# Fixed places for one chain of small steps in a two-layer cross attention, one unit combined in blocks, a lag of 116 steps in place of 124

## The chip, the cores and the metric

The kernel runs on one core of a Trainium2 chip. The metric is the time of one execution on the device in microseconds (us). TensorE (PE in the profile), VectorE (DVE), ScalarE (ACT), GpSimd (POOL) and SyncE (SP, which here only issues DMAs) run their own lists of instructions and meet at semaphores. A wait stands in its engine's list, so everything behind it in that list waits too.

## The reference

Two layers of cross attention with 20 heads of 16 columns, on 4 batches of 512 queries and 1024 keys. Everything is float32. Layer 0 is

```python
q, k_t, v_t = heads(x @ W_q), heads(text @ W_k), heads(text @ W_v)      # text: the first 1020 tokens
probs_t = softmax(q k_t / 4);  text_out = probs_t v_t
qsem = l2norm(probs_t @ text);  sem = qsem . l2norm(ip)                 # ip: the last 4 tokens
probs_ip = softmax(q k_ip / 4 + 0.5 * sem) * mask
x1 = (text_out + probs_ip v_ip) @ W_out + b_out + x
```

Layer 1 takes x1 and is simpler. It has two softmaxes, one over the first 77 tokens and one over the other 947 with other weights, and its output is (out_text + out_ip) @ Wo + bo + x1.

## The kernel before

**Units, groups, chunks.** A unit is one layer and one half batch of 256 queries (`UNITS`, line 52): units 0 to 7 are layer 0, units 8 to 15 are layer 1. `B` is 8, and `LAST` is unit 15. Unit 8 + b needs the output x1 of unit b. A unit has ten groups of two heads. A head has four chunks of 256 keys, so a unit has 80 chunks and the kernel has 1280. A chunk is scored on TensorE (the `score` step), ScalarE takes exp of it twice (`prob` and the rounded `prob_hi`), the difference `prob_lo` is formed on VectorE (layer 0, and one in eight of the tail) or on GpSimd (the rest of layer 1), and TensorE multiplies both parts with the values: `mix` in layer 0, which also forms the 512 columns of qsem, and `av1` in layer 1.

**The order.** `plan()` writes one list of steps, which all engines walk. `unit_sequence()` (line 62) interleaves the layers: layer 1 runs `LAG_UNITS` chunks behind layer 0. With 124 there are three phases: "lead" (124 chunks of layer 0 alone), "woven" (516 pairs of one chunk from each layer) and "tail" (chunks of layer 1 alone). I number the chunks of the whole order, n = 0 to 1279. Before, the tail begins with n = 1155 and has 125 chunks: 45 of unit 14 and the 80 of LAST. LAST begins at n = 1200, before and after. I write "tail + 8" for the eighth chunk after the tail's first one.

**Side work.** Between chunks `hook(limit)` takes up to `limit` steps, three in the tail: first what is in `urgent`, then `topq`, then `bgq`. `topq` is filled from `top_agenda`, a list by chunk number, which holds the maxima: for each group eight matmuls (`max`, line 1150) with a reduction on VectorE each (lines 1548, 1549 and 1551), then `neg`, `neg_parts` and `max_rows`, which put minus the row maxima beside the queries. A group's first score needs its `max_rows`. `bgq` is filled from `jobs` with deadlines, spread over windows of four chunks by `job_tasks()`. `put_off()` lets one small piece go per call of `hook`. `load_at` holds the places of `load_qk(g)`, which loads queries and keys of group g into a ring of five slots. If they aren't ready by then, `load_due()` runs the missing steps at once, all together. This happens once in the kernel before, at n = 1183 (tail + 28).

**The chain between the layers' last units.** When unit 7 ends, at the tail's start, these steps lead to LAST's queries: `combine` (lines 1606 to 1614), `fuse_root`, `fuse_exp` and `fuse_probs` (lines 1397, 1651 to 1688: the small softmax over four tokens), `probs_rows` (1257), three `turn` (1276, 1279, 1709, 1711), three `finish` (1297, 1719), `x_split` (1354, 1703) and three `q` (1176) with `split`, `split_hi` and `lower`, which cut q in three bf16 parts on VectorE and GpSimd and store them by DMA (1439 to 1449, 1737, 1743, 1835). `load_qk` of LAST's first group then reads them back (1870 to 1874). Before, these steps are a job in `bgq`. By the printed order `combine` stands at tail + 8 to + 10, `fuse_exp` at + 11 and + 12, `fuse_probs` up to + 16, `probs_rows` at + 17, `turn` at + 19 to + 24, `finish` at + 25 to + 27, `x_split`, the first `q`, its whole split and three `load_qk` together at + 28, the second `q` at + 32 and + 33, the maxima of LAST's first group at + 34 to + 39 with `max_rows` at + 40, its first score at + 42, and the third `q` at + 55.

**Unit 14.** After its last head (tail + 44) it is combined with seven put-off steps (lines 1610 to 1620, tail + 49 to + 51): two reciprocals, four multiplications of 320 columns and two additions of 320. LAST is combined in three blocks of 8, 8 and 4 heads (`combine_block`, lines 1632 to 1641), the first two while its heads are still running.

Of the kernel before, what the change touches and what calls it, by code (L numbers as in the profile page):

```python
# [7 lines left out]
ALU = mybir.AluOpType  # L8
# [7 lines left out]
HEADS = 20  # L16
# [4 lines left out]
SEM_SCALE = 0.5  # L21
LAG_UNITS = 124
WINDOW = 4
# [20 lines left out]
DH = D // HEADS  # L44
# [10 lines left out]
NU = NT // UNIT_KEYS  # L55
LAST = 2 * B - 1
BLOCKS = [(P * m // DH, (P * m + MW[m]) // DH) for m in range(NM)]
PER_GROUP = GROUP * NU
# [57 lines left out]
def plan():  # L116
# [280 lines left out]
    for g, (u, gi) in enumerate(seq):  # L397
        if g >= RING:
            done_at = end_of[g - RING] - (1 if end_of[g - RING] < woven else 2)
            at = max(done_at, start_of[g] - (25 if g < RING + 12 else 28 if start_of[g] < tail else 36))  # L400
            load_at.setdefault(max(at, start_of[place[(u, 0)]] - 16) if u == 2 * B - 1 else at, []).append(g)
        layer = UNITS[u][0]
        mine = [x for x in range(groups) if UNITS[seq[x][0]][0] == layer]
        i = mine.index(g)
        if i >= 2 or layer == 1:
            load_v_at.setdefault(max(end_of[mine[i - 2]] if i >= 2 else 0, start_of[g] - 24), []).append(g)
# [76 lines left out]
    def last_close():  # L483
# [9 lines left out]
        for m in range(NM):  # L493
            o.add("finish", LAST, m, NM - 1)

    def unit_done(u):
        layer, b = UNITS[u]
        if u == LAST:
            last_block(NM - 1)
            return  # L500
        put_off(*[("combine", u, i) for i in range(3 if layer == 0 else 7)])
        if layer == 0:
            add_job(project_q(B + b), due_of(B + b))
            if b + 2 < B:
                add_job(project_q(b + 2), due_of(b + 2))
            if b % PARTS == 1 and b + 3 < B:
                add_job(project_kv(b + 3), due_of(b + 3), "kv")
            if b % PARTS == 0 and b + 2 < B:
                add_job(project_kv(B + b + 2), due_of(B + b + 2), "kv")
        else:  # L510
            first, second = close(u)
            if u < LAST - 1:
                add_job(first + second, window_of(start_of[place[(u, 0)]] + 16 * PER_GROUP * NG // PER_GROUP))
            else:
                add_job(first + second, window_of(start_of[place[(LAST, 0)]] + 24))
# [41 lines left out]
    for g in range(1, groups):  # L557
        span, margin = MAX_SPAN[phase(start_of[g])]
        last_at = start_of[g] - margin
        if seq[g] == (2 * B - 1, 0):  # L560
# [27 lines left out]
    def rows_of(n):  # L588
        _, u, h, c = chunks[n]
        if n < 0 or UNITS[u][0] == 0 or c < NU - 1:  # L590
            return
        o.add("l1_rows", n)
        urgent.append((n + 3, lambda: turn_head(u, h)))
        if u == LAST and h + 1 in [end for _, end in BLOCKS[:-1]]:
            urgent.append((n + 5, lambda: last_block([end for _, end in BLOCKS].index(h + 1))))
        if h == HEADS - 1:
            urgent.append((n + 3, lambda: unit_done(u)))
# [44 lines left out]
    for n, (g, u, h, c) in enumerate(chunks):  # L642
# [22 lines left out]
        if layer == 0:  # L665
# [23 lines left out]
            if c == NU - 1:  # L689
                if h == 0:  # L690
                    drain()
                o.add("values", n, 0)
                values_due.append(n)
                if h == HEADS - 1:
                    urgent.append((n + 3, lambda u=u: unit_done(u)))
# [33 lines left out]
def cross_attention_pair(nc, a, out):  # L729
# [32 lines left out]
    with ctx:  # L762
# [149 lines left out]
        close0 = {s[1]: i for i, s in enumerate([s for s in o.steps if s[0] == "fuse_root"])}  # L912
        comb_base, comb_here, base = {}, {}, 0
        for s in o.steps:
# [5 lines left out]
            elif s[0] == "combine_block":  # L920
                comb_base.setdefault(s[1], base)
                base += 2 if s[3] == 0 else 1
        ip_nth = {s[1]: i for i, s in enumerate([s for s in o.steps if s[0] == "ip_norm"])}
        head_end = {(u, h): n for n, (g, u, h, c) in enumerate(chunks) if c == NU - 1}
# [109 lines left out]
        def _(e):  # L1034
# [16 lines left out]
            for s in o.steps:  # L1051
# [207 lines left out]
                elif kind == "turn":  # L1259
# [4 lines left out]
                    if k == 0:  # L1264
                        e.wait_ge(s_comb, comb_base[u] + (5 * (m + 1) if u == LAST else COMBINED[layer]))
                        if layer == 0:
# [136 lines left out]
        def _(e):  # L1403
            for x, rows in ((x_in[1], high_rows), (o_t[1], low_rows)):
                e.memset(x.bitcast(F32)[rows, NM - 1, :], 0.0).then_inc(s_pad, 1)
            for s in o.steps:
# [214 lines left out]
                elif kind == "combine_block":  # L1621
                    _, u, m, piece = s
                    h0, h1 = BLOCKS[m]
                    i0 = comb_base[u] + 5 * m
                    ho = heads_out[1][:, :, h0:h1, :]
# [7 lines left out]
                    elif piece == 1:  # L1633
                        e.wait_ge(s_comb, i0 + 1)
                        e.tensor_tensor(at, ho[:, :, :, 0:DH], wide[0], ALU.mult).then_inc(s_comb, 1)
                    elif piece == 2:
                        e.wait_ge(s_comb, i0 + 2)
                        e.tensor_tensor(image, image, wide[1], ALU.mult).then_inc(s_comb, 1)
                    else:
                        e.wait_ge(s_comb, i0 + 4)  # L1640
                        e.tensor_tensor(at, at, image, ALU.add).then_inc(s_comb, 1)
                elif kind == "fuse_exp":
                    _, u, piece = s
# [121 lines left out]
        def _(e):  # L1765
            for s in o.steps:
# [137 lines left out]
                elif kind == "residual":  # L1904
                    _, u, m = s
                    layer, b = UNITS[u]
                    w, nth_close = MW[m], close_nth[u]
                    e.wait_ge(s_comb, comb_base[u] + (5 if u == LAST else COMBINED[layer]))
                    if nth_close:
# [58 lines left out]
```

## Time and profile before

| | us |
|---|---|
| median of 3 runs | 3438.0 (3437.28 to 3439.05) |
| the profiled execution's own time | 3436.6 |
| its span in the trace | 3434.8 |
| TensorE busy | 3332.4 (97%) |
| VectorE, ScalarE, GpSimd busy | 1994.1, 1832.6, 1089.5 |

Busy times are those of the span. An engine's busy share doesn't say what the end waits for, so the page's slices come next, and then the trace of the last 200 us. A line number is that of the kernel before.

### The profile page before, as it was taken

How to read it: one execution, taken by the hardware profiler on the slowest of the kernel's cores; microseconds unless marked ns; L12 is line 12 of the kernel's file. 1: busy time of each engine (PE TensorE's matmuls, PEld its weight loads, DVE VectorE, ACT ScalarE, POOL GpSimd, SP SyncE). 2: the span in 40 equal slices, each digit the busy share in tenths (PEclk: the TensorE clock that was granted, in tenths of full speed). 3: DMA queues.
4: the chain of work that ended last, by engine and by line, in shares of the span. 5: the costliest groups of instructions: out<-in, count | busy, mean ns of one | idle time of the engine just before them, and what ended most of it. 6: DMA issues, size and time to landing. Idle time of an engine off the chain costs nothing.

```text
span 3434.8 us, 65575 instructions
## 1 busy us (share of the span) xinstructions
PE 3332.4 (97%) x24736; PEld 2893.0 (84%) x24736; DVE 1994.1 (58%) x5511; ACT 1832.6 (53%) x4006; POOL 1089.5 (32%) x932
## 2 busy tenths in 40 slices
PE   6999999999999999999999999999999999999978
PEld 3888978887888888888888888888888898989755
DVE  4444455556655566565656556655665556555677
ACT  2333334555555555555655555555565566565668
POOL 2111010234332333333433232333423322322368
PEclk8999999999999999999999999999999999999989
DMA  6333822233358332233347432323327532222232
GB/s 186 108 87 71 97 84 76 62 80 90 86 79 105 77 74 68 75 92 81 92 72 72 98 73 68 78 72 104 90 68 76 67 59 51 59 47 53 49 79 57
DMA packets 648781, 271.28 MB, mean 79 GB/s; under 512 B 479666, under 2 KB 599426, under 8 KB 648468
## 3 DMA queue, kind: packets, MB, share of 16 engines
q1 hardware_dynamic: 648468, 267.10, 38.0%
q8 instruction: 198, 3.24, 0.4%
q14 instruction: 115, 0.94, 0.1%
HBM read 187.97 MB, written 79.04 MB: 78 GB/s over the span
## 4 chain that ended last, share of the span: by engine, by line
PE 88%; DVE 5%; ACT 3%; POOL 1%; issue 1%; DMA 1%; SPq 1%; POOLq 0%; ACTq 0%; DVEq 0%
PE acc L1106 9%; PE acc L1099 9%; PE acc L1102 8%; PE acc L1101 8%; PE acc L1107 8%; PE acc L1100 7%; PE score L1066 4%; PE spare L1150 4%; PE score L1150 4%; PE score L1068 4%; PE av L1141 3%; PE av L1137 3%; PE spare L1191 2%; PE score L1191 2%; PE score L1240 2%; PE spare L1240 2%
## 5 line engine op out<-in xcount | busy, mean ns | idle before, releaser
L1317 ACT ACTIVATE prob<-score 128x512 f32<-128x512 f32 x1219 | 729.1, 598 | 1194.2 <-PE score L1068 1189.0
L1731 POOL TENSOR_TENSOR prob_lo<-prob,prob_hi 128x512 fp32r<-128x512 f32 x624 | 811.9, 1305 | 1487.3 <-ACT prob_hi L1320 1486.8
L1099 PE MATMUL acc<-tok_v,prob_hi 128*128 128x300 f32 x2240 | 908.6, 406 | 0.9 <-issue 0.9
L1101 PE MATMUL acc<-tok_lo,prob_hi 128*128 128x256 f32 (+1 forms) x2560 | 757.9, 296 | 0.0
L1106 PE MATMUL acc<-tok_v,prob_lo 128*128 128x278 f32 (+1 forms) x2560 | 745.5, 291 | 0.0
L1320 ACT ACTIVATE prob_hi<-score 128x512 fp32r<-128x512 f32 x1219 | 726.2, 596 | 0.0
L1102 PE MATMUL acc<-tok_lo,prob_hi 128*128 128x256 f32 (+1 forms) x2560 | 719.0, 281 | 0.0
L1107 PE MATMUL acc<-tok_v,prob_lo 128*128 128x256 f32 (+1 forms) x2560 | 717.8, 280 | 0.0
L1100 PE MATMUL acc<-tok_v,prob_hi 128*128 128x256 f32 x2240 | 627.6, 280 | 0.0
L1102 PEld LDWEIGHTS acc<-tok_lo,prob_hi 128*128 128x128 f32 (+1 forms) x2560 | 483.6, 189 | 7.4 <-issue 1.4
L1101 PEld LDWEIGHTS acc<-tok_lo,prob_hi 128*128 128x128 f32 (+1 forms) x2560 | 484.4, 189 | 4.1 <-issue 1.8
L1106 PEld LDWEIGHTS acc<-tok_v,prob_lo 128*128 128x128 f32 (+1 forms) x2560 | 482.4, 188 | 0.0
L1107 PEld LDWEIGHTS acc<-tok_v,prob_lo 128*128 128x128 f32 (+1 forms) x2560 | 481.7, 188 | 0.0
L1430 DVE TENSOR_TENSOR prob_lo<-prob,prob_hi 128x512 fp32r<-128x512 f32 x656 | 461.9, 704 | 30.4 <-ACT prob_hi L1320 29.7
L1099 PEld LDWEIGHTS acc<-tok_v,prob_hi 128*128 128x128 f32 x2240 | 427.9, 191 | 44.4 <-issue 20.2
L1100 PEld LDWEIGHTS acc<-tok_v,prob_hi 128*128 128x128 f32 x2240 | 427.7, 191 | 35.1 <-issue 17.2
L1066 PE MATMUL score<-q_ring,k_ring 99*128 99x256 bf16 (+1 forms) x1219 | 337.9, 277 | 15.1 <-ACT prob_hi L1320 14.3
L1068 PE MATMUL score<-q_ring,k_ring 99*128 99x256 bf16 (+1 forms) x1219 | 330.9, 271 | 0.0
L1137 PE MATMUL av<-prob_hi,v_ring 128*33 128x256 f32 (+1 forms) x1152 | 273.2, 318 | 4.1 <-issue 4.1
L1150 PE MATMUL spare<-k_ring,q_ring 96*128 96x512 bf16 x605 | 237.3, 392 | 5.6 <-DVE max_parts L1551 2.6
L1141 PE MATMUL av<-prob_lo,v_ring 128*33 128x256 f32 (+1 forms) x1152 | 230.5, 281 | 5.5 <-POOL prob_lo L1731 4.5
L1150 PE MATMUL score<-k_ring,q_ring 96*128 96x512 bf16 x586 | 229.8, 392 | 4.4 <-DVE max_parts L1549 2.3
(323 smaller groups left out, 4963.5 us busy)
## 6 DMA issues: line engine op xcount, KB each, us to landing
k_ring<-k_scr SPq DMA_DIRECT2D x160, 384.0 KB
tok_v<-v_scr SPq DMA_DIRECT2D x158, 176.0 KB, 3.4
v_ring<-v_scr SPq DMA_DIRECT2D x160, 148.5 KB, 3.4
ctx_t<-in_ctxT SPq DMA_DIRECT2D x16, 1024.0 KB, 8.7
q_ring<-q_scr SPq DMA_DIRECT2D x160, 96.0 KB
v_scr<-v_stage SPq DMA_DIRECT2D x32, 440.0 KB, 2.6
v_scr<-v_stage SPq DMA_DIRECT2D x36, 330.0 KB, 9.3
tok_stage<-in_ctx SPq DMA_DIRECT2D x32, 256.0 KB, 3.0
```

The source lines that it names most:

```text
L1066: e.matmul(score[n][:, 0:SQ], k_ring[0:depth, slot, j, 2 * c * P:(2 * c + 1) * P], queries, start=True, stop=True)
L1068: e.matmul(score[n][:, SQ:2 * SQ], k_ring[0:depth, slot, j, (2 * c + 1) * P:(2 * c + 2) * P], queries, start=True, stop=True).then_inc(s_s ...
L1099: e.matmul(out_a[:, 0:SEG + VCOLS], p_hi, tok_v[0:kk, c, seg, v_lo:v_lo + SEG + VCOLS], start=first, stop=False)
L1100: e.matmul(out_b[:, t0:t0 + SEG], p_hi, tok_v[0:kk, c, 1 - seg, VCOLS:VCOLS + SEG], start=first, stop=False)
L1101: e.matmul(out_a[:, t0:t0 + SEG], p_hi, tok_lo[0:kk, c, seg * SEG:(seg + 1) * SEG], start=False, stop=False)
L1102: e.matmul(out_b[:, t0:t0 + SEG], p_hi, tok_lo[0:kk, c, (1 - seg) * SEG:(2 - seg) * SEG], start=False, stop=False)
L1106: e.matmul(out_a[:, v_one:v_one + SEG + VH], p_lo, tok_v[0:kk, c, seg, v_lo + v_one:v_lo + v_one + SEG + VH], start=False, stop=False)
L1107: mm = e.matmul(out_b[:, t0:t0 + SEG], p_lo, tok_v[0:kk, c, 1 - seg, VCOLS:VCOLS + SEG], start=False, stop=False)
L1150: e.matmul(bg[:, :], q_ring[0:96, slot, j, st * P:(st + 1) * P], k_ring[0:96, slot, j, half * 512:(half + 1) * 512], start=True, stop=True ...
L1317: e.activation(prob[:, es, :], bank_s[:, :], ACT.Exp, scale=SCALE)
L1320: e.activation(prob_hi[:, ps, :], bank_s[:, :], ACT.Exp, scale=SCALE).then_inc(s_exp, 1)
L1731: e.tensor_tensor(prob_lo[:, ps, :], prob[:, es, :], prob_hi.bitcast(F32)[:, ps, :], ALU.subtract).then_inc(s_low[1], 1)
```

## The change

It has five parts. First, `LAG_UNITS` is 116: lead 116 chunks, woven 524 pairs, tail 117 chunks (n = 1163 to 1279), 37 of them of unit 14. Second, the chain above is no job any more. `last_chain()` puts each step at a fixed chunk: `combine` 0, `fuse_root` and two `fuse_exp` at tail + 1, the other two at + 2, `combine` 1 and `fuse_probs` 0 at + 3, `combine` 2 and `fuse_probs` 1 at + 4, `fuse_probs` 2 at + 5, the residual loads at + 6, `probs_rows` at + 7, `turn` at + 8 to + 10, `finish` at + 11 to + 13, `x_split` at + 15, `q` at + 17 to + 19. Third, unit 14 is combined in blocks like LAST, but the additions are done at the end, as two `combine_sum` steps of 320 columns each, since `attn` still holds unit 7 when the blocks begin. Fourth, the maxima of unit 14's groups that start in the tail are due 11 chunks ahead of the group's start in place of 14. Fifth, LAST's loads of queries and keys stand 12 chunks ahead of its start at the earliest in place of 16 (n = 1188), and those of unit 8, the first of layer 1, at most 14 ahead.

```diff
-LAG_UNITS = 124
+LAG_UNITS = 116
+BY_BLOCKS = (LAST - 1, LAST)
...
-            load_at.setdefault(max(at, start_of[place[(u, 0)]] - 16) if u == 2 * B - 1 else at, []).append(g)
+            load_at.setdefault(max(at, start_of[place[(u, 0)]] - (12 if u == LAST else 14)) if u in (B, LAST) else at, []).append(g)
...
+    def last_chain():
+
+        u = B - 1
+        tasks = [t for t in project_q(LAST) if not isinstance(t, Pause)]
+        root, exps, (ask, total, probs), rows = tasks[0], tasks[2:6], tasks[7:10], tasks[11]
+        (res0, res1, res2), turns, finishes = tasks[12:15], tasks[15:18], tasks[18:21]
+        x_split, q = tasks[22], tasks[23:]
...
+        places = [(0, several(lambda: combine(0), root, *exps[0:2])), (1, several(*exps[2:4])),
+                  (2, several(lambda: combine(1), ask)), (3, several(lambda: combine(2), total)), (4, probs),
+                  (5, several(res0, res1, res2)), (6, rows)]
+        places += [(7 + m, turns[m]) for m in range(NM)] + [(10 + m, finishes[m]) for m in range(NM)]
+        places += [(14, x_split)] + [(16 + m, q[m]) for m in range(NM)]
+        for at, task in reversed(places):
+            top_agenda.setdefault(now[0] + 2 + at, []).insert(0, task)
...
-        put_off(*[("combine", u, i) for i in range(3 if layer == 0 else 7)])
+        if u in BY_BLOCKS:
+            put_off(*[("combine_block", u, NM - 1, i) for i in range(3)], *[("combine_sum", u, st) for st in range(ST)])
+        else:
+            put_off(*[("combine", u, i) for i in range(3 if layer == 0 else 7)])
...
-        last_at = start_of[g] - margin
+        last_at = start_of[g] - (11 if start_of[g] >= tail and seq[g][0] == LAST - 1 else margin)
...
-        if u == LAST and h + 1 in [end for _, end in BLOCKS[:-1]]:
-            urgent.append((n + 5, lambda: last_block([end for _, end in BLOCKS].index(h + 1))))
+        if u in BY_BLOCKS and h + 1 in [end for _, end in BLOCKS[:-1]]:
+            m = [end for _, end in BLOCKS].index(h + 1)
+            if u == LAST:
+                urgent.append((n + 5, lambda: last_block(m)))
+            else:
+                urgent.append((n + 5, lambda: put_off(*[("combine_block", u, m, i) for i in range(3)])))
...
-                if h == HEADS - 1:
+                if u == B - 1 and h == HEADS - 1:
+                    last_chain()
+                elif h == HEADS - 1:
                     urgent.append((n + 3, lambda u=u: unit_done(u)))
...
+                        text = ho[:, :, :, 0:DH]
+                        e.tensor_tensor(at if u == LAST else text, text, wide[0], ALU.mult).then_inc(s_comb, 1)
...
+                elif kind == "combine_sum":
+                    _, u, st = s
+                    ho = heads_out[1][:, st, :, :]
+                    e.wait_ge(s_comb, comb_base[u, NM - 1] + 4)
+                    e.tensor_tensor(attn[:, st, :, :], ho[:, :, 0:DH], ho[:, :, DH:2 * DH], ALU.add).then_inc(s_comb, 1)
```

The rest of the diff keeps count of the semaphore `s_comb` for the blocks of two units.

## Rows read from the trace of the kernel before

**Rows 1.** The page: busy time by engine; TensorE and its granted clock in 40 slices.
```profile
PE 3332.4 (97%) x24736; PEld 2893.0 (84%) x24736; DVE 1994.1 (58%) x5511; ACT 1832.6 (53%) x4006; POOL 1089.5 (32%) x932
...
PE   6999999999999999999999999999999999999978
...
PEclk8999999999999999999999999999999999999989
```

**Rows 2.** Windows of the tail: stretch, length, busy time of each engine, clock, DMA.
```profile
core 0: us, PE busy (x) PEld busy (x) DVE busy (x) ACT busy (x) POOL busy (x), PEclk, DMA share, GB/s
...
3245.00:3267.00 22.00, 14.19 (x81) 8.64 (x81) 21.03 (x59) 15.81 (x31) 12.82 (x11) 0.84 0.15 30
...
3287.00:3297.00 10.00, 7.73 (x55) 6.35 (x56) 2.45 (x8) 5.75 (x12) 6.76 (x6) 0.83 0.35 96
3297.00:3305.00 8.00, 3.87 (x29) 2.60 (x28) 5.18 (x11) 4.88 (x10) 7.27 (x7) 0.88 1.03 212
...
3327.00:3334.00 7.00, 1.95 (x9) 0.98 (x8) 6.90 (x12) 1.47 (x5) 3.97 (x3) 0.75 0.56 123
...
3341.00:3398.00 57.00, 53.14 (x390) 35.19 (x389) 54.14 (x163) 54.51 (x114) 53.70 (x43) 1.00 0.38 75
```

**Rows 3.** TensorE's timeline: `av1` of tail + 0, 5, 18, 29, 45, 61, 105.
```profile
3236.40 0.48 PE L1137 MATMUL av<-prob_hi,v_ring 128*33 128x256 f32 x2
...
3241.35 0.48 PE L1137 MATMUL av<-prob_hi,v_ring 128*66 128x256 f32 x2
...
3267.85 0.48 PE L1137 MATMUL acc<-prob_hi,v_ring 128*33 128x256 f32 x2
...
3288.03 0.48 PE L1137 MATMUL av<-prob_hi,v_ring 128*66 128x256 f32 x2
...
3316.86 0.48 PE L1137 MATMUL av<-prob_hi,v_ring 128*66 128x256 f32 x2
...
3345.31 0.47 PE L1137 MATMUL av<-prob_hi,v_ring 128*66 128x256 f32 x2
...
3398.48 0.48 PE L1137 MATMUL acc<-prob_hi,v_ring 128*66 128x256 f32 x2
```

**Rows 4.** TensorE's waits from 3236 to 3340: total us, times, longest.
```profile
PE acc L1150 <- DVE heads_out L1593: 4.9, 1, 4.9
PE av L1137 <- issue: 4.1, 1, 4.1
...
PE spare L1150 <- DVE max_parts L1551: 2.6, 1, 2.6
PE spare L1176 <- DVE x_in_lo L1703: 2.6, 1, 2.6
```

**Rows 5.** Windows, VectorE alone, of tiles `max_parts`, `small` and `w`.
```profile
3245.00:3267.00 22.00, 8.75 (x22) 0.84 0.15 30
...
3245.00:3268.00 23.00, 8.05 (x14) 0.85 0.15 29
...
3245.00:3268.00 23.00, 1.82 (x4) 0.85 0.15 29
```

**Rows 6.** VectorE's timeline: unit 14's combination, first and last of its rows.
```profile
3324.13 0.40 DVE L1610 RECIPROCAL small<-heads_out 128x40 f32<-128x40 f32 x1
...
3328.30 3.02 DVE L1617 TENSOR_TENSOR heads_out<-heads_out,small 128x320 f32<-128x320 f32 x2
3331.35 1.02 DVE L1620 TENSOR_TENSOR attn<-attn,heads_out 128x320 f32<-128x320 f32 x2
```

**Rows 7.** One line over the span: shortest, median and longest duration in ns.
```profile
L1614 DVE TENSOR_TENSOR attn<-heads_out,small x30: 472/482/1599, 430.7 to 3327.4; 128x320 f32<-128x320 f32 x30
...
L1638 DVE TENSOR_TENSOR heads_out<-heads_out,small x3: 286/1494/1497, 3413.4 to 3428.0; 128x256 f32<-128x256 f32 x2, 128x128 f32<-128x128 f32 x1
```

**Rows 8.** Timelines of SP's queue and TensorE: LAST's first group, load, maximum, score.
```profile
3293.49 0.28 SPq L1870 DMA_DIRECT2D k_ring<-row_scr  x1
...
3297.85 0.39 PE L1150 MATMUL score<-k_ring,q_ring 96*128 96x512 bf16 x1
...
3313.70 0.27 PE L1066 MATMUL score<-q_ring,k_ring 102*128 102x256 bf16 x1
```

More of the change, by code:

```diff
@@ L494, in last_close, with combine, several, go @@
             o.add("finish", LAST, m, NM - 1)
+    def last_chain():
[4 more added lines that the diff above has]
+        x_split, q = tasks[22], tasks[23:]
+        def combine(i):
+            o.add("combine", u, i)
+        def several(*tasks):
+            def go():
+                for task in tasks:
+                    task()
+            return go
+        places = [(0, several(lambda: combine(0), root, *exps[0:2])), (1, several(*exps[2:4])),
[5 more added lines that the diff above has]
+            top_agenda.setdefault(now[0] + 2 + at, []).insert(0, task)
     def unit_done(u):
@@ L912, in cross_attention_pair @@
         close0 = {s[1]: i for i, s in enumerate([s for s in o.steps if s[0] == "fuse_root"])}
-        comb_base, comb_here, base = {}, {}, 0
+        comb_base, comb_done, comb_here, base = {}, {}, {}, 0
         for s in o.steps:
@@ L920, in cross_attention_pair @@
             elif s[0] == "combine_block":
-                comb_base.setdefault(s[1], base)
+                comb_base.setdefault(s[1:3], base)
                 base += 2 if s[3] == 0 else 1
+                comb_done[s[1:3]] = base
+            elif s[0] == "combine_sum":
+                base += 1
+                comb_done[s[1], NM - 1] = base
         ip_nth = {s[1]: i for i, s in enumerate([s for s in o.steps if s[0] == "ip_norm"])}
@@ L1264, in _ @@
                     if k == 0:
-                        e.wait_ge(s_comb, comb_base[u] + (5 * (m + 1) if u == LAST else COMBINED[layer]))
+                        e.wait_ge(s_comb, comb_done[u, m if u == LAST else NM - 1] if u in BY_BLOCKS else comb_base[u] + COMBINED[layer])
                         if layer == 0:
@@ L1623, in _ @@
                     h0, h1 = BLOCKS[m]
-                    i0 = comb_base[u] + 5 * m
+                    i0 = comb_base[u, m]
                     ho = heads_out[1][:, :, h0:h1, :]
@@ L1634, in _ @@
                         e.wait_ge(s_comb, i0 + 1)
-                        e.tensor_tensor(at, ho[:, :, :, 0:DH], wide[0], ALU.mult).then_inc(s_comb, 1)
+                        text = ho[:, :, :, 0:DH]
+                        e.tensor_tensor(at if u == LAST else text, text, wide[0], ALU.mult).then_inc(s_comb, 1)
                     elif piece == 2:
@@ L1907, in _ @@
                     w, nth_close = MW[m], close_nth[u]
-                    e.wait_ge(s_comb, comb_base[u] + (5 if u == LAST else COMBINED[layer]))
+                    e.wait_ge(s_comb, comb_done[u, 0 if u == LAST else NM - 1] if u in BY_BLOCKS else comb_base[u] + COMBINED[layer])
                     if nth_close:
```

## The prediction, made before the changed kernel was built

> **What bounds the kernel now.** I read the page's busy times and slices first [rows 1]. TensorE is busy 97% of the span, and its slices are all at 9 except the first and the last two. So until the tail the kernel is bound by TensorE's own work, and an edit that only moves work about in the woven phase gives nothing there. The last two slices stand at 7 and 8 with a lower clock, and the whole change acts on them.
>
> Then I read the tail's windows and its chunks. `av1` of the tail's first chunk starts at 3236.40 and of tail + 45, LAST's first chunk, at 3316.86 [rows 3]: 80.5 us for 45 chunks, 1.79 each. From tail + 61 to + 105 it is 53.17 us for 44 chunks, 1.21 each, with ScalarE busy 54.51 of 57 us, VectorE 54.14 and GpSimd 53.70 [rows 2, 3]. All three are full there, so 1.21 is the tail's free pace. The first five chunks take 4.95 us, 0.99 each [rows 3]: that is TensorE's own pace, since the scores are ahead. At 1.21 the 45 chunks would take 54.5 us, so 26 us are lost before LAST starts. Another 9.1 us are lost in the 16 chunks behind it (28.45 us in place of 19.4).
>
> The losses have four places. (1) From 3245 to 3267 VectorE is busy 21.03 of 22 us [rows 2], with both the maxima and the chain's small steps. (2) TensorE waits 2.6 us for `x_split`'s low part, which stands right ahead of `q` in the bunch that `load_due()` forces, and 4.1 us at an `av1`, just when SP issues the loads of three groups ahead of the values; DMA is at 1.03 in that window [rows 2, 4]. (3) The clock falls to 0.83 and 0.88 of full between 3287 and 3305 [rows 2]. (4) TensorE waits 4.9 us for `heads_out` while VectorE combines unit 14: it is busy 1.95 of 7 us there and VectorE 6.90 [rows 2, 4].
>
> **The change part by part.** I sum against the profiled execution: span 3434.8, 3436.6 with what lies around it, 1.4 under the median.
>
> *Eight chunks leave the tail for the woven phase.* There each costs TensorE's pace, 8 x 0.99 = +7.9 us. The same chunks and side work remain in total, and the lead phase loses eight chunks of layer 0 that become halves of pairs, at the same TensorE work. What they cost in the tail is in the stretches below. Below nothing this can't be, since TensorE is at 9 in nearly every slice there; its upper bound is the tail's free pace, 8 x 1.21 = 9.7.
>
> *Stretch A, the tail's start to `probs_rows`.* Before it was 18 chunks and 31.45 us, 3236.40 to 3267.85 [rows 3]. After it is 7 chunks. VectorE sets it. Its chain steps cost 8.05 us on `small` and 1.82 on `w`, with one operation of 0.3 in both: 9.5 us [rows 5]. The rest of VectorE's 21.03 us, 11.5 us, belongs to the ten chunks from tail + 8 to + 18, 1.15 each, 8.75 of it maxima [rows 2, 5]. Seven chunks then make 7 x 1.15 + 9.5 = 17.6, and I take 18. It can't be under 17.0 (nothing is left out of the chain and the maxima go on at one per chunk; their later due time takes three at most away). The upper bound is 24: the steps now stand back to back, and TensorE, in order, may wait at a bank for a maximum that stands behind three of them.
>
> *Stretch B, from there to the first `q`.* Eleven chunks before (20.2 us, 3267.85 to 3288.03 [rows 3]) and eleven after. `x_split` now stands two chunks ahead of `q`, which covers 2 x 1.21 us of work; since side steps slip by a chunk or so when more than three are due, I take half of the 2.6 us wait [rows 4]. The maxima of the unit's last two groups now lie beside it, which I put at +0.5. 19.4 us; bounds 17.6 (the wait wholly gone) and 23 (as before, and four maxima more at 0.7).
>
> *Stretch C, from there to LAST's first chunk.* 16 chunks before and 28.8 us; 19 after. At the free pace 23.0. The 4.1 us at `av1` go: the values of the group that waited are loaded ahead of the three `load_qk` now, not behind. What is late next is LAST's first group. Its load stands nine chunks ahead of the step that scores it: 10.9 us of cover. In the trace, load to first maximum is 4.4 us and load to first score 20.2 [rows 8], of which 4.1 is that wait. The least is 4.4 + 8 x 0.73 (maxima at 8.75 us for some twelve [rows 5]) = 10.2, the most 16.1. So TensorE waits between 0 and 5.2 us for `max_rows`; 3.4, above the middle, because all eight maxima become due in one chunk. Block 1 of unit 14's combination lands here too, where VectorE is busy 2.45 of 10 us [rows 2]: nothing; without that cover it would cost its some 3 us (two operations of 1.5 [rows 7]). C is 26.4; bounds 23.0 and 33.
>
> A + B + C = 63.8 in place of 80.5: -16.7 us.
>
> *Unit 14 in blocks.* Before, its steps fill VectorE from 3324.13 to 3332.4, 8.2 us [rows 6]. After, the last four heads and two sums remain: two small reciprocals (under 0.4 each, by that of 40 columns), two multiplications of 128 columns (0.29 at the shortest, 1.50 at the longest [rows 7]) and two sums (1.02 for both in rows 6, up to 1.6 each [rows 7]). That makes 1.9 to 7.0 us; I take 3.0, near the short end, as the sums were at 0.5 in this same place. So -5.2; bounds -6.3 and -1.2. What is late behind it is the free pace. The block of the first eight heads falls into the woven phase, where VectorE has 40% free.
>
> The same operation takes 472 ns at the shortest and 1599 at the longest [rows 7], and the long ones lie where GpSimd is full. The Trainium skill, GPSIMD Engine Reference, Specifications, says that GpSimd shares its SBUF interfaces with VectorE and collides with operations of two SBUF inputs; all of the combination's multiplications and sums are such. By that rule the last block alone would take up to 7.0 us in the tail, and the sum would come out 4 us higher. The row with 472 ns shows that it isn't so each time. The rule is one of the reasons for the first rival.
>
> *The rest.* The loads of unit 8 change nothing, since their deadline falls on the same window as before (chunk 100, now 102). From LAST's seventeenth chunk on, the order of steps stays, and its 89.5 us with it.
>
> Sum: 7.9 - 16.7 - 5.2 = -14.0. The execution comes to 3422.6, the median to 3424.0 us.
>
> **The rivals.** *The chain stays in-order bound.* Packing the steps doesn't make VectorE faster; TensorE waits at more banks and more `max_rows`, and GpSimd stretches the two-input operations. Against it: VectorE is busy only 2.45 of 10 and 5.18 of 8 us from 3287 to 3305 [rows 2], which the fixed places can fill. A = 24, B = 22, C = 29 give 75, -5.5; blocks -5.2; +7.9: -2.8, that is 3435.
>
> *Slower: LAST's first group comes late.* Place: `max_rows` of LAST's first group, scored nine chunks behind its loads in place of thirteen. If load to score takes the 20.2 us of rows 8 in place of the cover's 10.9, TensorE waits 9.3 us. With the loads behind the stores of the second and third `q` on SP's queue, A = 26 and B = 24 (a little above their bounds, for the lower clock behind long waits) and C = 23.0 + 3.7 for these stores + 9.3 = 36, the tail's first part takes 86 us: +5.5 + 7.9 - 5.2 = +8.2, 3446. It decides from 85 us between the tail's first chunk and LAST's first. For it speaks that DMA was full when these loads ran [rows 2]; against it that the bunch then held three groups and values behind a forced `q`, all of which are apart now.
>
> *More than forecast.* The stalls go nearly all: A + B + C at 37 x 1.21 + 9.5 = 54, -26.5; -5.2; +7.9: -24, 3414. It needs VectorE to work the chain wholly beside the chunks, while it has 2.9 of 57 us free at that pace [rows 2].
>
> *It doesn't do what it says.* The fixed places are places in `topq`, and three steps per chunk are let through. With maxima, head turns and chain that is passed from tail + 8 on, so steps may slip two to three chunks. That costs no more than the first rival and is in it.
>
> **How the numbers follow.** Forecast 3424, chance 0.58, with an own range of 3418 to 3431. First rival 3435: 0.19. Slower 3446: 0.11. More 3414: 0.12. Some 7 us (0.2%) is about what a measurement of this kernel can tell from no change, so faster ends at 3431 and slower begins at 3445: faster 0.70, same 0.19, slower 0.11. The range leaves out the slower rival and a part of the best one: 3413 to 3438.
>
> **What would show it.** In the trace of the changed kernel: 117 `av1` behind the last `mix`; LAST's first chunk 60 to 68 us after the tail's first, `probs_rows` near 18 us; the wait of 4.1 us at `av1` and that of 4.9 us for `heads_out` gone; a wait of `max_rows` of 2 to 5 us right ahead of LAST; clock above 0.9 but for single windows; unit 14's last block and sums in 2 to 4 us; the pace from then on 1.21 us per chunk and the last 64 chunks in 89.5 us. The forecast is wrong if the first stretch takes over 24 us, if LAST's first score comes later than 85 us, or if the woven phase grows by more than 9.7 us.

## The result, and the profile after

The changed kernel takes 3475.6 us (median of 4 runs, 3467.7 to 3476.9) against 3438.5 (3437.3 to 3439.9) before: a ratio of 1.0104 with an interval of 1.0091 to 1.0116. It is slower by 37 us, where 14 faster was forecast. The profiled execution took 3476.9 us, its span is 3475.1. The page of the changed kernel, busy times and TensorE's slices:

```profile
PE 3354.0 (97%) x24736; PEld 2905.7 (84%) x24736; DVE 1991.3 (57%) x5516; ACT 1835.8 (53%) x4006; POOL 1094.0 (31%) x933
...
PE   6999999999999999999999999999999999999978
...
PEclk8999999999999999999999999999999999999989
```

Against [rows 1] nothing is to be seen but 22 us more of TensorE. So I cut the order at steps that mean the same in both kernels: layer 0's chunk 124 (counted from 0), the tail's first chunk and LAST's first one. I give all kernels of this study by this cut, in us from the span's start to chunk 124, from there to the tail, from the tail to LAST, and from LAST's first chunk to its last output matmul.

| kernel | median | ratio to before, interval | to chunk 124 | to the tail | to LAST | LAST |
|---|---|---|---|---|---|---|
| before | 3438.5 | | 629.4 | 2607.0 | 80.5 | 114.6 |
| after | 3475.6 | 1.0104 (1.0091 to 1.0116) | 637.5 | 2650.4 | 73.1 | 110.8 |
| `lag116_alone` | 3479.0 | 1.0120 (1.0105 to 1.0135) | 636.5 | 2654.4 | 74.9 | 113.1 |
| `lag116_no_blocks` | 3472.3 | 1.0103 (1.0085 to 1.0121) | 636.6 | 2643.6 | 74.0 | 112.1 |
| `lag116_kv_as_before` | 3458.3 | 1.0058 (1.0043 to 1.0072) | 637.9 | 2631.2 | 72.8 | 110.3 |
| `lag116_late_loads` | 3443.6 | 1.0016 (1.0007 to 1.0026) | 637.4 | 2618.2 | 70.8 | 110.7 |
| `lag116_late_due14` | 3434.9 | 0.9988 (0.9979 to 0.9998) | 637.0 | 2618.6 | 63.2 | 110.8 |
| `lag116_late_due14_kv` | 3433.0 | 0.9984 (0.9976 to 0.9993) | 636.9 | 2614.1 | 63.8 | 112.0 |
| `lag120_due14` | 3446.8 | 1.0024 (1.0015 to 1.0033) | 627.9 | 2624.9 | 78.5 | 110.6 |
| `lag124_chain_only` | 3433.7 | 0.9987 (0.9977 to 0.9996) | 630.0 | 2607.1 | 79.6 | 113.7 |
| `lag124_unit8_loads` | 3432.9 | 0.9987 (0.9977 to 0.9996) | 620.4 | 2612.1 | 82.9 | 114.8 |
| `lag124_rest_new` | 3430.1 | 0.9975 (0.9966 to 0.9985) | 619.7 | 2611.7 | 82.6 | 112.3 |
| `lag124_due14` | 3427.6 | 0.9969 (0.9957 to 0.9981) | 620.7 | 2612.0 | 77.4 | 112.0 |
| `lag128_due14` | 3460.4 | 1.0064 (1.0050 to 1.0078) | 625.0 | 2630.3 | 90.1 | 111.5 |

Between before and after these four stretches differ by 8.1 + 43.4 - 7.4 - 3.8 = 40.3 us, which is the growth of the span. The 8.1 us up to chunk 124 are the forecast 7.9 for eight chunks woven in. The 43.4 us behind it (43.3 by the windows below), in a stretch where the same work runs in both, had no term. Medians are of several executions, but each stretch is of one profiled execution. Three of the kernels (after, `lag116_alone` and `lag116_no_blocks`) have the same printed order up to chunk n = 1144, nearly the whole woven stretch, and still take 2650.4, 2654.4 and 2643.6 us there. So differences of ten us between woven stretches can be chance.

**The woven stretch.** Its window, first of the kernel before, then of after (length; busy time of TensorE, its loads, VectorE, ScalarE, GpSimd; clock, DMA):

```profile
629.40:3236.40 2607.00, 2585.46 (x19668) 2279.12 (x19667) 1541.69 (x4266) 1465.61 (x3196) 856.86 (x717) 1.00 0.37 75
```

```profile
638.00:3288.30 2650.30, 2603.09 (x19665) 2288.67 (x19664) 1540.05 (x4266) 1466.91 (x3195) 858.55 (x717) 0.99 0.37 74
```

The number of matmuls is the same, but for three that a trace misses. TensorE is idle for 47.2 us in place of 21.5, and busy 17.6 us longer for the same work. Its longest waits in that stretch, before and after (line waited at, what released it; total us, times, longest):

```profile
PE score L1066 <- ACT prob_hi L1320: 12.0, 13, 1.2
PE spare L1150 <- DVE max_parts L1549: 2.6, 4, 0.8
PE score L1150 <- DVE max_parts L1549: 1.9, 3, 0.7
```

```profile
PE score L1104 <- ACT prob_hi L1358: 19.8, 10, 6.0
PE score L1214 <- DVE x_in_lo L1747: 6.4, 3, 2.1
PE spare L1214 <- DVE x_in_lo L1747: 4.4, 2, 2.3
PE spare L1188 <- DVE max_parts L1587: 2.7, 5, 0.8
PE score L1288 <- DVE closing L1763: 2.5, 1, 2.5
```

Two kinds are new: five waits of a unit's first `q` for the low part of x, and two long waits (6.0 and 4.9 us) of a score for ScalarE.

*The first kind.* The timeline of after where unit 9 gets its queries:

```profile
907.81 0.93 ACT L1392 ACTIVATE x_in_hi<-closing 128x512 fp32r<-128x512 f32 x2
...
908.47 1.68 DVE L1747 TENSOR_TENSOR x_in_lo<-closing,x_in_hi 128x512 fp32r<-128x512 f32 x2 [1.54 <-ACT x_in_hi L1392]
...
910.41 0.47 PE L1214 MATMUL score<-x_in_hi,wq_parts 128*128 128x256 f32 x2 [2.12 <-DVE x_in_lo L1747]
```

`q` stands directly behind `x_split` in the list, so TensorE, in order, waits until ScalarE and VectorE have split all of x. By the printed order, before one step of mixing stood between the two only for unit 8, and 5 to 30 for units 9 to 14. After it is one for all but unit 10, which has four and is the one that doesn't wait. The woven phase has six such chains, one for each unit b of layer 0 whose x1 makes unit 8 + b's queries. The deadline of each is the load of unit 8 + b's first group. A lag of 116 puts that load 22 chunks of layer 0 behind the end of unit b (and the first score 35), where 124 puts it at 30 (and 43). To meet it, the job runs without room between its steps; run 4 below tests this.

*The second kind.* ScalarE at a border between batches, where the tokens of the next batch are read and split, and SP's queue ahead of it:

```profile
1682.13 0.63 ACT L1408 ACTIVATE tok_v<-tok_stage 128x512 fp32r<-128x512 f32 x1 [5.01 <-DMA tok_stage<-in_ctx]
...
1669.36 1.59 SPq L1943 DMA_DIRECT2D tok_stage<-in_ctx  x2
1671.49 0.53 SPq L1900 DMA_DIRECT2D v_scr<-v_stage  x1
1674.40 1.57 SPq L1943 DMA_DIRECT2D tok_stage<-in_ctx  x2
1676.08 0.29 SPq L1914 DMA_DIRECT2D k_ring<-row_scr  x1
1676.41 0.33 SPq L1916 DMA_DIRECT2D k_ring<-k_scr  x1
1676.78 2.42 SPq L1918 DMA_DIRECT2D q_ring<-q_scr  x1
```

And in the kernel before, at the same border:

```profile
1630.21 7.00 SPq L1899 DMA_DIRECT2D tok_stage<-in_ctx  x4
```

Before, all four token reads stand together; after, a store of values (`v_scr`) stands among them, since unit 12's value job now runs from layer 0's chunk 296 to 329 in place of 340 to 368, over the border at 317 to 320. ScalarE waits 5.0 us for a read, the exp of the next chunks stand behind that wait on its list, and TensorE waits 6.0 us for `prob_hi`. The same happens at 2535 us with unit 14. That the value jobs bring it is shown by run 5. What in them makes the read late isn't: the store ahead of it in the queue took 10.4 us to land, but the second pair of reads was also issued only 5.0 us after the first.

*The clock.* Windows of after around two of these waits (same columns):

```profile
905.00:912.00 7.00, 4.88 (x40) 4.55 (x40) 4.25 (x14) 3.44 (x8) 1.27 (x1) 0.99 0.35 62
912.00:916.00 4.00, 4.00 (x24) 3.99 (x24) 0.97 (x4) 1.41 (x3) 0.00 (x0) 0.59 0.00 0
1680.00:1687.00 7.00, 1.04 (x5) 0.79 (x5) 1.07 (x2) 3.37 (x9) 3.75 (x3) 0.74 0.65 150
1687.00:1691.00 4.00, 4.00 (x18) 3.38 (x17) 1.27 (x7) 1.92 (x4) 2.52 (x3) 0.61 0.64 144
```

Behind the wait TensorE is busy without a break, at a clock near 0.6, that is mostly at 1.2 GHz. The trace has seven stretches at 1.2 GHz in the woven phase after, 30.7 us in all, and none before: four at waits for the low part, two at the waits for ScalarE, and one at the wait of 2.5 us for `closing`. TensorE is busy in 25.8 of these us; at half speed half of that is lost, some 12.9 of the 17.6 us that it was busy longer. So the 43.3 us are 25.7 of waiting and 17.6 of slower work, and most of the second goes with the first.

### The profile page after: what moved, and what is told of

The parts are those of the page before. It is cut to its first block, busy times and chain, and to the rows that moved or that the text cites. A ratio compares the mean times of both kernels' runs of the same rounds, so it can differ in the third digit from the quotient of the medians.

```text
span 3475.1 us, 65594 instructions
## 1 busy us (share of the span) xinstructions
PE 3354.0 (97%) x24736; PEld 2905.7 (84%) x24736; DVE 1991.3 (57%) x5516; ACT 1835.8 (53%) x4006; POOL 1094.0 (31%) x933
## 4 chain that ended last, share of the span: by engine, by line
PE 86%; DVE 5%; ACT 2%; DMA 2%; issue 1%; SPq 1%; POOL 1%; POOLq 0%; DVEq 0%; ACTq 0%
PE acc L1144 9%; PE acc L1137 9%; PE acc L1139 8%; PE acc L1140 8%; PE acc L1145 8%; PE acc L1138 7%; PE score L1104 4%; PE spare L1188 4%; PE score L1188 4%; PE score L1106 4%; PE av L1175 3%; PE av L1179 3%; PE spare L1229 2%; PE score L1229 2%; PE score L1278 2%; PE spare L1278 2%
```

## The experiments

All start from the changed kernel, unless "before" is named. The times are in the table above.

**1. `lag124_rest_new`: everything but the lag.**

```diff
-LAG_UNITS = 116
+LAG_UNITS = 124
```

> The changed kernel with the lag set back to 124, all else of the change kept. Theory S (the shorter lag squeezes the chain from unit b to unit 8+b in every unit of the woven phase, so that each q stands right behind its x_split and TensorE waits and drops to the lower clock; the tail's edits are sound): the 2 us waits of the first q for x_in_lo in the woven phase are gone, at most one stretch of half clock there, tail begins at 3236 +- 3, and the time is 3438 less most of the 11 us that the changed tail gained: 3425 to 3433. Rival T (the other edits, the blocks above all, cost the woven phase its 43 us): 3465 or more.

3430.1 us. The woven stretch falls from 2650.4 to 2611.7 us, its waits for `prob_hi` are 11.6 us, and it has no stretch at 1.2 GHz. The other four parts together gain 0.25% (interval 0.15 to 0.34), and the lag costs 45 us on top of them, of which 17.8 lie ahead of chunk 124: 8 for the chunks woven in, and a gain of unit 8's loads that only the longer lag has (run 6).

**2. `lag116_alone`: before, with the lag and the rule for unit 8's loads.**

```diff
-LAG_UNITS = 124
+LAG_UNITS = 116
...
-            load_at.setdefault(max(at, start_of[place[(u, 0)]] - 16) if u == 2 * B - 1 else at, []).append(g)
+            load_at.setdefault(max(at, start_of[place[(u, 0)]] - (16 if u == LAST else 14)) if u in (B, LAST) else at, []).append(g)
```

> The kernel before with the lag of 116 and only the rule for unit 8's loads that this lag needs; chain, combination and maxima as before. Theory S: the woven phase loses its 40 to 45 us here too, with the q waits at x_in_lo and half-clock stretches; the tail has the forced bunch at tail + 20, so in all 3478 to 3495. Rival T: 3430 to 3445.

3479.0 us: the lag alone brings the whole loss, with the same waits and the same stretches at 1.2 GHz in the woven phase. Eight chunks fewer make the way from the tail to LAST only 5.6 us shorter (74.9 in place of 80.5).

**3. `lag116_no_blocks`: unit 14 combined whole.**

```diff
-BY_BLOCKS = (LAST - 1, LAST)
+BY_BLOCKS = (LAST,)
```

> The changed kernel with unit 14 combined whole as before. Theory S: the woven phase as in the changed kernel; behind LAST's first chunk the combination of 7 to 8 us on VectorE and a wait of TensorE for a head turn or a maximum of 4 to 5 us are back: 3476 + 2 to 6 us. Rival T: the woven phase is back at the level of before, 3430 to 3445.

3472.3 us, whose interval overlaps the changed kernel's, where I had expected 2 to 6 more. TensorE's wait ahead of the maxima of LAST's third group is 3.8 us in place of 2.5, and the tail as a whole is 2.2 us longer (186.1 in place of 183.9). The forecast 5.2 us aren't there. Two of this run's five waits for the low part were followed by a stretch at 1.2 GHz, where after has four.

**4. `lag116_late_loads`: the loads of units 9 to 14 at most 16 chunks ahead.**

```diff
-            load_at.setdefault(max(at, start_of[place[(u, 0)]] - (12 if u == LAST else 14)) if u in (B, LAST) else at, []).append(g)
+            load_at.setdefault(max(at, start_of[place[(u, 0)]] - (12 if u == LAST else 14 if u == B else 16)) if u >= B else at, []).append(g)
```

> The changed kernel with the loads of units 9 to 14 held until 16 steps ahead of the unit's first chunk, which moves their jobs' deadlines back by six chunks of layer 0, so that x_split and q stand apart as with the lag of 124. Theory S: the waits for x_in_lo in the woven phase fall from six of 2.1 us to one or two, half-clock stretches from eight to three or fewer, and the time to 3430 to 3450. Rival U (the half clock and the waits come from DMA at the batches' borders and not from the squeezed chain): 3465 or more, with the waits of 5 to 6 us of score for prob_hi left and the clock still low behind them.

3443.6 us, 32 fewer, all of it in the woven stretch (2618.2). The load now stands 28 chunks behind the end of unit b in place of 22, with 4 to 30 steps of mixing between `x_split` and `q` of units 9 to 14. The waits at `q` are gone from the list of the woven stretch, one stretch at 1.2 GHz is left, and TensorE is busy 2589.6 us. The deadline of the chain was the cause, not the chunks that moved. But which of the two kinds of wait weighs how much can't be told from it, since the same edit moves the value jobs of units 12 and 14 back behind the borders (from chunks 340 and 488). The next run parts the two. Some 11 us of the 43 stay here (2618.2 us against 2607.0), and 7 in run 11; no run says where they come from.

**5. `lag116_kv_as_before`: only the key and value jobs of units 12 and 14 moved back.**

```diff
-                add_job(project_kv(B + b + 2), due_of(B + b + 2), "kv")
+                add_job(([Pause(10)] if b else []) + project_kv(B + b + 2), due_of(B + b + 2), "kv")
```

> The changed kernel, where the jobs for the keys and values of units 12 and 14 are held back ten windows, so that they run beside the same chunks of layer 0 as in the kernel before (keys 300 to 320 and 460 to 480, values 340 to 364 and 500 to 535) and no longer across the batches' borders at 317 to 320 and 477 to 480. The q chains stay squeezed. Two-cause theory (waits of 6.0 and 4.9 us of score for prob_hi at the borders, and the squeezed q chains with 2 us each, are separate): the two border waits and their 13.6 us of half clock go, the six q waits stay, and the time falls by 14 to 24 us, to 3452 to 3462. Rival (the squeezed chain causes both): 3470 or more. Rival (the borders are nearly all): under 3448.

3458.3 us, 17 fewer, within the 14 to 24 of the theory with two causes. The woven stretch of this kernel, and its first waits:

```profile
638.10:3269.40 2631.30, 2592.73 (x19665) 2281.18 (x19664) 1548.35 (x4266) 1468.65 (x3195) 857.82 (x717) 1.00 0.36 74
```

```profile
PE score L1104 <- ACT prob_hi L1358: 9.2, 9, 1.3
PE score L1214 <- DVE x_in_lo L1747: 8.5, 4, 2.1
PE spare L1214 <- DVE x_in_lo L1747: 4.2, 2, 2.1
```

The two long waits for ScalarE are gone, and the six at `q` are all there, 12.7 us. They are followed by only one stretch at 1.2 GHz (at 910 us), where the changed kernel had four behind its five. So what a wait of 2.1 us brings behind it isn't settled by its length alone.

**6. `lag124_unit8_loads`: before, with unit 8's loads at most 14 chunks ahead.**

```diff
-            load_at.setdefault(max(at, start_of[place[(u, 0)]] - 16) if u == 2 * B - 1 else at, []).append(g)
+            load_at.setdefault(max(at, start_of[place[(u, 0)]] - (16 if u == LAST else 14)) if u in (B, LAST) else at, []).append(g)
```

> The kernel before with one edit alone: unit 8's loads of queries and keys at most 14 steps ahead. Theory E (of the 8 us that the changed kernel gains at a lag of 124, the part before the tail, 5 us in the profiled runs, comes from this rule, because unit 8's chain stops being packed behind one deadline): layer 0's chunk 100 starts near 506 us in place of 526, the tail at 3231 to 3233, and the time is 3430 to 3434. Rival (it is the tail's edits or chance): 3437 to 3440.

3432.9 us, a gain of 0.13% (0.04 to 0.23). Chunk 124 comes 9.0 us earlier, and 5.1 of them come back in the woven stretch. The waits of TensorE from 300 to 510 us in the kernel before were these; with the rule there are none.

```profile
PE av L1161 <- DVE row_parts L1582: 2.6, 2, 1.6
PE av L1176 <- DVE x_in_lo L1703: 1.3, 1, 1.3
PE av L1297 <- DVE o_t_lo L1711: 0.2, 1, 0.2
```

By the printed order the rule moves unit 8's first load from 19 to 30 chunks of layer 0 behind the end of unit 0, and 20 steps of mixing then stand between `x_split` and `q` in place of one. With a lag of 116 the same rule leaves `x_split` at chunk 96 and one step of mixing, as before, and the changed kernel has the same waits from 300 to 510 us: 4.0 us in place of 4.1.

**7. `lag116_late_due14`: run 4, with unit 14's last maxima due 14 chunks ahead, as before.**

```diff
-        last_at = start_of[g] - (11 if start_of[g] >= tail and seq[g][0] == LAST - 1 else margin)
+        last_at = start_of[g] - margin
```

> lag116_late_loads with unit 14's maxima due 14 chunks ahead as before, not 11. Theory M (the later due time makes max_rows of the last groups late, 3.2 us of wait at the group 149): that wait falls under 1 us, and the time is 3 us less, near 3440. Rival N (VectorE has the same maxima in either case and the wait only moves to the chain): within 1.5 us of 3443.6, with a longer stretch from the tail's start to probs_rows than 18.4 us.

3434.9 us, 8.7 fewer than run 4, where I had put 3. From the tail to LAST it is 63.2 us in place of 70.8. The wait that goes is that of `max_rows` for group 149, unit 14's last, 3.2 us in the changed kernel; the clock's stretches at 1.2 GHz in the tail up to LAST shrink from 17 us (run 4) to 10. By the printed order `neg`, `neg_parts` and `max_rows` of this group stand in one chunk (tail + 25), right ahead of its first score, when the maxima are due 11 ahead; with 14, `neg` stands four chunks ahead. This part of the change costs time.

**8. `lag124_chain_only`: before, with the fixed places alone** (`last_chain()` as in the diff ahead of the prediction).

> The kernel before with the fixed places for the chain alone (lag 124, unit 14 combined whole, maxima due 14 ahead, loads of LAST as before, no rule for unit 8). Theory P (with 45 chunks to go through before LAST the stretch is bound by VectorE and ScalarE work, not by the chain's latency, so an earlier chain gains little): tail to LAST's first chunk 78 to 83 us, time 3434 to 3439. Rival L (the chain was what LAST waited for): 70 us or less and 3428 or less.

3433.7 us, a gain of 0.13% (0.04 to 0.23). `probs_rows` comes at 16.6 us in place of 31.1, the first `q` at 39.2 in place of 50.5, but LAST's first chunk only 0.9 us earlier (79.6). The time goes back in waits, among them those of `max_rows` for groups 149, 150 and 151 (1.8, 2.0 and 2.2 us, the last one behind LAST's first chunk), each with a stretch at 1.2 GHz beside it. The fixed places take the chain off the path, and the maxima take it over.

**9. `lag124_due14`: run 1 with run 7's edit.**

> All of the change but the lag (124 stays), and unit 14's last maxima due 14 steps ahead, as before the change, in place of 11. Theory (the later due place only makes TensorE wait at the last maxima, and each such wait is followed by a stretch at 1.2 GHz): the stretch from the tail's start to the last unit's first chunk falls from 82.6 us to 74 to 79, and the median from 3430.1 to 3422 to 3427. Rival (what the 116-step kernel gained by it, 8.7 us by its span, came from the places that steps took there by chance): within 2 us of 3430.1.

3427.6 us, the fastest of the study: 0.31% under before (0.19 to 0.43). The way from tail to LAST falls from 82.6 to 77.4 us, within the 74 to 79 of the theory, though the median falls by only 2.5, half a microsecond short of the forecast band, and the span by 4.3.

**10. `lag120_due14`: the same with a lag of 120.**

> The same with a lag of 120. Theory (the eight chains from a unit of layer 0 to layer 1's unit lose half of the room that 116 steps take): between the two, chunks moved into the woven phase add 4 us there and take 4 to 6 off the tail, and waits of TensorE of more than 1.3 us ahead of queries appear in at most some units: 3420 to 3432. Rival (any cut of the room brings the waits of 2 us and the stretches at 1.2 GHz back): three or more stretches at 1.2 GHz in the woven phase and over 3440.

3446.8 us, over the theory's 3432. The rival has the time right, but not its reason: there is one stretch at 1.2 GHz in the woven phase, and two waits of 2.1 us at `q`. What is new are waits of maxima:

```profile
PE score L1188 <- DVE max_parts L1581: 4.5, 4, 1.5
PE spare L1214 <- DVE x_in_lo L1747: 4.3, 2, 2.1
PE spare L1188 <- DVE max_parts L1581: 3.0, 3, 1.3
```

**11. `lag116_late_due14_kv`: run 7 and run 5's pause together.**

> The change with the loads of units 9 to 14 held to 16 steps ahead, unit 14's last maxima due 14 steps ahead, and a pause of 10 chunks ahead of the key and value jobs of units 12 and 14. Theory (held loads and moved value jobs are two remedies for the same waits, so the second finds little left): 3431 to 3437, beside 3434.9 without the pauses; the two stretches at 1.2 GHz in the woven phase (near 1911 and 2311 us) go or stay one. Rival (each takes away waits of its own): below 3430.

3433.0 us. The median is 1.9 us lower, within overlapping intervals, and the stretches at 1.2 GHz near 1911 and 2311 us are gone. As expected the second remedy finds little left. So held loads had mended both kinds of wait.

**12. `lag128_due14`: run 9 with a lag of 128.**

> All of the change but the lag, which is 128, and unit 14's last maxima due 14 steps ahead. By its printed order only three to six steps of mixing stand between a unit's low part of x and its first query (one at 116, 5 to 30 at 124, 1 to 25 at 120). Theory (those steps are what hides the low part; each such place without cover costs up to 2.1 us, and four chunks go back from the woven phase to the tail, 4 us less there and 5 to 7 more here): waits at the queries of 0.5 to 1.5 us at four or more units, 3428 to 3438, over the 3427.6 of lag 124. Rival (a longer lag only gives the chains more room, whatever stands where): no waits over 0.5 us at the queries, and 3427 to 3431.

3460.4 us, over both expectations. The queries don't wait more (0.9 us at one unit), though only three to six steps of mixing hide the low part; so few are enough, and one is not. The woven stretch is 18 us longer than with 124 for another reason, and the tail 13 us. Its waits of maxima:

```profile
PE spare L1188 <- DVE max_parts L1581: 4.3, 3, 1.5
PE score L1188 <- DVE max_parts L1581: 4.1, 3, 1.5
PE spare L1188 <- DVE max_parts L1587: 3.0, 2, 1.8
PE score L1199 <- DVE row_parts L1620: 2.8, 2, 2.2
```

At 124 the waits at line 1188 in the woven stretch come to 5.1 us with 0.8 at the longest; at 120 they are 12.7, at 128 15.4. At these lags the maxima of layer 1 fall beside other steps of layer 0. Which ones, no run parts.

## Why the prediction was wrong

**Eight chunks to the woven phase (+7.9).** The step that failed. The eight chunks themselves cost 8.1 us, as worked out. What was put at nothing behind them measures 43.4. What I wrote behind it, "its upper bound is the tail's free pace, 9.7", bounded the chunks that move and not what a new lag does to the rest. The lag is the distance between unit b and unit 8 + b in every place, so it shortens six more chains and the jobs filed with them, not only the one that the change gives fixed places. My first reading, that an edit which only moves work in the woven phase gives nothing, since TensorE is at 9 in every slice [rows 1], took a busy engine for one that can't be delayed. It was already idle 21.5 us there, in 2607. What the slices can't show is how near each hand-over stands. I had listed the chain's places only for unit 7, and the same list for units 1 to 6 would have shown one step of cover in place of 5 to 30 (four for unit 10). That wait was in my rows too: `x_in_lo`, 2.6 us [rows 4], for just that standing, `q` right behind `x_split`.

**Stretch A (18).** `probs_rows` comes 18.4 us behind the tail's first chunk, but that was luck in part: the fixed places are places in the queue, and steps slipped behind the maxima. By the printed order and the trace `probs_rows` runs at tail + 9 and not + 7, and the sum's own prices give 19.9 us for nine chunks. **Stretch B (19.4)** took 22.2, within its bounds of 17.6 to 23, for twelve chunks and not eleven: `x_split` runs at tail + 20 (place + 15) and the three `q` at + 21, + 24 and + 25 (places + 17 to + 19). So one chunk stood between `x_split` and `q`, not two, and the wait for the low part came at 2.0 us with a first matmul at half clock. **Stretch C (26.4)** took 32.5, at its upper bound of 33, though only 16 chunks were left for it in place of 19. At the free pace they are 19.4 us, so 13 us were lost where the sum had 3.4. Timeline of after, the `av1` of the tail's first chunk, the first `q`, and LAST's first `av1`:

```profile
3287.86 0.47 PE L1175 MATMUL av<-prob_hi,v_ring 128*33 128x256 f32 x2
...
3328.46 0.71 PE L1214 MATMUL score<-x_in_hi,wq_parts 128*128 128x256 f32 x2 [2.04 <-DVE x_in_lo L1747]
...
3360.92 0.48 PE L1175 MATMUL av<-prob_hi,v_ring 128*66 128x256 f32 x2
```

A, B and C are 73.1 in place of 63.8 us. The largest mis-sized term is that of the maxima due later: "at + 0.5", where run 7 measures 7.6. TensorE's waits in the tail of after:

```profile
PE acc L1199 <- DVE row_parts L1620: 3.4, 2, 3.2
PE score L1199 <- DVE row_parts L1620: 2.6, 1, 2.6
...
PE spare L1188 <- DVE heads_out L1631: 2.5, 1, 2.5
PE spare L1199 <- DVE row_parts L1620: 2.2, 1, 2.2
PE score L1214 <- DVE x_in_lo L1747: 2.0, 1, 2.0
```

The wait of 4.1 us at `av1` is gone, as forecast. In place of two `max_rows` waits of 1.4 and 1.3 us (groups 150 and 151) there are three, of 3.2, 2.6 and 2.2 us, for groups 149, 150 and 151; the last one is behind LAST's first chunk, as before. And I had costed waits without the clock behind them: windows of the tail of after show 0.73 to 0.89 where I had forecast over 0.9.

```profile
3308.00:3330.00 22.00, 19.70 (x137) 16.52 (x136) 13.70 (x40) 15.78 (x32) 13.96 (x11) 0.89 0.24 44
3330.00:3345.00 15.00, 11.12 (x72) 8.57 (x71) 9.15 (x27) 8.12 (x16) 9.01 (x11) 0.73 0.38 106
3345.00:3362.00 17.00, 12.70 (x77) 7.84 (x76) 13.54 (x33) 10.61 (x23) 11.08 (x10) 0.88 0.63 137
```

**Unit 14 in blocks (-5.2).** TensorE's wait for `heads_out` fell from 4.9 us [rows 4] to 2.5, and LAST's first 16 chunks take 28.0 in place of 28.45 us, so most of the term is absent. VectorE and GpSimd in after:

```profile
3368.21 0.27 DVE L1670 RECIPROCAL small<-heads_out 128x8 f32<-128x8 f32 x2
...
3369.07 0.28 DVE L1674 TENSOR_TENSOR heads_out<-heads_out,small 128x128 f32<-128x128 f32 x1
...
3370.06 0.74 DVE L1677 TENSOR_TENSOR heads_out<-heads_out,small 128x128 f32<-128x128 f32 x1
3370.83 2.92 DVE L1685 TENSOR_TENSOR attn<-heads_out 128x320 f32<-128x320 f32 x2
```

```profile
3369.36 5.51 POOL L1775 TENSOR_TENSOR prob_lo<-prob,prob_hi 128x512 fp32r<-128x512 f32 x4 [1.91 <-ACT prob_hi L1358]
```

Reciprocals, multiplications and sums are 4.2 us in place of 3.0, and with maxima among them they hold VectorE from 3368.2 to 3373.8. The two sums, which I had put at 0.5 each, took 1.45 and 1.55, beside four `prob_lo` of GpSimd without a pause. In the kernel before, GpSimd had just ended when the same two sums took 1.02 together, from 3331.35 on [rows 6]:

```profile
3325.27 5.70 POOL L1731 TENSOR_TENSOR prob_lo<-prob,prob_hi 128x512 fp32r<-128x512 f32 x4 [1.33 <-ACT prob_hi L1320]
```

So the sums at 0.5 each were a price from an idle GpSimd. The Trainium skill, GPSIMD Engine Reference, Specifications, says that GpSimd shares its SBUF interfaces with VectorE, with contention for VectorE's instructions of two SBUF inputs; the sums are such, and the trace agrees.

**The loads of unit 8 (nothing).** Right for this change: with a lag of 116 the steps and the waits stay as they were. At 124 the same rule gives 9.0 us up to chunk 124 (run 6), which the forecast hadn't looked for. **LAST behind its seventeenth chunk** took 82.8 in place of 86.2 us, a small gain that I hadn't. Of it 1.8 us lie in the 44 chunks behind the seventeenth. They take 51.3 to 51.7 us in every kernel with the fixed places and 52.5 to 53.2 in the three without, so it comes with them, and why stays open. Another 1.5 us are in the last 20 chunks, 31.5 in place of 33.0, and that is luck: before had a stretch of 3.4 us at 1.2 GHz at 3402, after has none (see the last section).

**The rivals.** The slower one was worked out for the wrong place: LAST's first group decided nothing at 73 us. "It doesn't do what it says" was right in that steps slip, by two to six chunks where it had put two to three. What I had named as a sign did tell: "the forecast is wrong if the woven phase grows by more than 9.7 us". It grew by 51, and no rival stood behind that sign.

## What to carry to other kernels

Before a distance that belongs to a whole schedule is changed, list for every instance what stands between producer and consumer on the in-order engine, not only for the instance one means to help: here one step of cover in place of 5 to 30 cost 2.1 us at each of them, and with the moved value jobs it took more than the whole gain of the tail. A slice that reads "busy 9 of 10" says that an engine has work, not that it can't be made to wait. When steps are given fixed places, look at what else has its deadline by the same number, since moved jobs meet other work (here token reads on SP's queue).

## What the runs showed of the hardware

I hadn't expected that TensorE's clock falls for a wait as short as these. After a single wait of 2.12 us (at 910, 1778, 2198 and 3000 us of the changed kernel), with TensorE busy without a break on both sides, a stretch of some 3.4 us at 1.2 GHz followed. At the waits of 6.0 and 4.9 the stretch was 6.8 us and began before the wait's end. It isn't certain: the wait of 2.3 us at 2623 had none behind it, nor had five of the six waits of 2.12 us in run 5. The same five waits in the same printed order were followed by four such stretches in after and in `lag116_alone`, and by two in `lag116_no_blocks`.

What one stretch costs can be read in LAST's last 20 chunks, where all 14 kernels have the same wait of 1.8 us for `o_t_lo`. In ten profiles a stretch of 3.4 us at 1.2 GHz starts within 1.3 us of the end of this wait, and these chunks take 32.9 to 33.1 us; in the other four there is none, and they take 31.5. So a stretch cost 1.5 us at this place, and a wait of 2.1 us costs 2.1 or some 3.6 (an estimate from these rows). Which one it is can't be told beforehand from these traces.
